# Half of an expert's output product in three rounded products, and bias transfers on another queue

## The reference

```
probs = softmax(x @ gate_w.T);  top2_p, top2_i = top_k(probs, 2)      # 14 experts
w   = top2_p / max(sum(top2_p), 1e-10)
hh  = gelu(x @ w1[e] + b1[e])                                         # w1: 512 x 1024
all_out[e] = hh @ w2[e] + b2[e]                                       # w2: 1024 x 512
result = clip(x + w[:, 0] * all_out[top2_i[:, 0]] + w[:, 1] * all_out[top2_i[:, 1]], -100, 100)
```

## Time and profile before

| what | value |
|---|---|
| runs | 486.13 us median of 3 (485.48 to 486.16) |
| profiled execution | 490.43 us, span from first to last instruction 488.6 us |
| TensorE busy | 452.6 us (93%) |
| VectorE, ScalarE, GpSimd busy | 280.4 us (57%), 162.3 us (33%), 49.8 us (10%) |
| mean granted clock of TensorE | 0.97 of full speed |
| HBM read and written | 93.98 MB and 21.50 MB, 236 GB/s over the span |

### The profile page before, as it was taken

How to read it: one execution, slowest core, us unless ns; L and a number is a source line. 1 busy time by engine, 2 the same in 40 slices (tenths; PEclk the granted TensorE clock), 3 DMA queues, 4 the chain that set the end, 5 groups by cost and what they waited for, 6 DMA issues and landing times.

```text
span 488.6 us, 8054 instructions
## 1 busy us (share of the span) xinstructions
PE 452.6 (93%) x3103; PEld 330.1 (68%) x3112; DVE 280.4 (57%) x555; ACT 162.3 (33%) x314; POOL 49.8 (10%) x58
## 2 busy tenths in 40 slices
PE   2797999999999999997999898999999999999983
PEld 1464665689898999986767766666666666666562
DVE  5639477874363133259565885566665555556637
ACT  4153135133332023043313443423344444333100
POOL 1300000001321111012030420000000000000062
PEclk9989899999999999999998999999999999999987
DMA  8987499004999638000613386899999999984452
GB/s 270 403 322 247 143 395 333 2 1 150 407 406 406 268 132 323 1 3 0 254 52 105 141 260 224 302 331 363 371 345 340 325 349 341 339 323 162 175 160 99
DMA packets 52382, 116.95 MB, mean 239 GB/s; under 512 B 4834, under 2 KB 4850, under 8 KB 52352
## 3 DMA queue, kind: packets, MB, share of 16 engines
q1 hardware_dynamic: 25984, 67.12, 36.8%
q10 hardware_dynamic: 24800, 44.62, 26.2%
q0 software_dynamic: 1568, 4.79, 3.1%
HBM read 93.98 MB, written 21.50 MB: 236 GB/s over the span
## 4 chain that ended last, share of the span: by engine, by line
PE 81%; DVE 12%; issue 2%; DMA 2%; POOL 1%; ACT 1%; DVEq 0%; ACTq 0%; POOLq 0%
PE banks L1780 17%; PE banks L1547 8%; PE banks L1759 5%; PE banks L1761 5%; PE banks L1760 5%; PE banks L1611 4%; PE banks L1413 3%; PE banks L1381 3%; PE banks L1414 3%; PE banks L1415 3%; PE banks L1452 3%; PE banks L1629 2%; PE banks L1400 2%; PE banks L1771 2%; PE banks L1580 2%
## 5 line engine op out<-in xcount | busy, mean ns | idle before, releaser
L1780 PE MATMUL banks<-w,A 128*128 128x512 f32 x208 | 91.4, 592 | 0.0
L670 ACT ACTIVATE A<-banks,b_sb 128x128 f32<-128x128 f32 x112 | 30.5, 383 | 115.5 <-issue 52.8
L1780 PEld LDWEIGHTS banks<-w,A 128*128 128x128 f32 x208 | 38.6, 190 | 43.6 <-issue 43.5
L1285 DVE COPY A<-banks 128x512 f32<-128x512 f32 x28 | 18.0, 686 | 68.0 <-PE banks L1761 67.8
L1213 DVE TENSOR_TENSOR w_lo<-w,w_hi 128x1024 fp32r<-128x1024 f32 x48 | 55.4, 1217 | 0.0
L1547 PE MATMUL banks<-A,w 128*128 128x128 f32 x384 | 48.1, 283 | 0.0
L603 ACT ACTIVATE w_hi<-w 128x1024 fp32r<-128x1024 f32 x48 | 47.3, 1094 | 0.8 <-ACT A L670 0.8
L1547 PEld LDWEIGHTS banks<-A,w 128*128 128x128 f32 x384 | 45.7, 198 | 0.7
L1759 PE MATMUL banks<-w_hi,xr 128*128 128x512 f32 x100 | 40.1, 401 | 1.5 <-DVE xr L1230 1.5
L1760 PE MATMUL banks<-w_lo,xr 128*128 128x512 f32 x104 | 40.5, 389 | 0.0
L1761 PE MATMUL banks<-w_hi,xr 128*128 128x512 f32 x100 | 39.0, 390 | 0.0
(11 more groups left out here) (288 smaller groups left out, 769.4 us busy)
## 6 DMA issues: line engine op xcount, KB each, us to landing
w<-in_w SPq DMA_DIRECT2D x12, 2048.0 KB, 10.1
w<-in_w ACTq DMA_DIRECT2D x12, 2048.0 KB, 10.7
rows_dram<-att ACTq DMA_DIRECT2D x1, 14592.0 KB, 43.1
A<-in_ctxT SPq DMA_DIRECT2D x8, 1024.0 KB, 10.4
A<-in_ctx SPq DMA_DIRECT2D x8, 1024.0 KB, 8.7
w<-in_w SPq DMA_DIRECT2D x6, 1024.0 KB, 6.1
rows_dram<-A ACTq DMA_DIRECT2D x13, 256.0 KB, 3.3
w<-in_wlT SPq DMA_DIRECT2D x3, 1024.0 KB, 15.1
```

Of the source, the lines that this page charges most:

```text
L670: ins = nc.scalar.activation(hT[:, u, f, :], HT[f // 4][:, tile(f % 4)], ACT.Gelu, bias=b1_sb[:, u, f:f + 1])
L1780: ins = mm(YP[:, :], hT[:, u, f, :], w2[:, u, f * D:(f + 1) * D], start=(f == 0), stop=(f == FT - 1))
```

## The change

In `output`, from block 2 on, tiles 4 to 7 of the 8 stay plain fp32 and tiles 0 to 3 (`G = 4`) become three rounded products each, added into the same bank behind the plain ones. For that the first half of `hT` and of `w2` are split: ScalarE rounds them (`high_w2`, and a copy at the end of `gelu`), VectorE subtracts (`low_w2`, `low_h`). In ScalarE's round `high_w2(b-1)` stands between `split_hi(b)` and `store_y(b-2)`; in VectorE's round `low_w2(b-1)` and `low_h(b-1)` stand between `take_y(b-2)` and `take_h(b)`. The issues of `b1` go from SyncE's and ScalarE's programs to GpSimd's, before its gathers.

```diff
+        G = FT // 2
+        w2_hi = [wqkv_lo_flat[:, 0:G * D], c_hi[:, :, :].rearrange("p k n -> p (k n)")[:, 0:G * D]]
+        h_hi = A2r[:, 1024:2048].rearrange("p (u f n) -> p u f n", u=2, f=G)
+        h_lo = A2r[:, 3072:5120].rearrange("p (u f n) -> p u f n", u=2, f=FT)[:, :, 0:G, :]
@@ SyncE @@
-            sp.dma_start(b1_sb[:, 0, :], t["b1T"][0]).then_inc(b1_in[0], 16)
...
-            sp.dma_start(b1_sb[:, 1, :], t["b1T"][1]).then_inc(b1_in[1], 16)
@@ ScalarE @@
+                    if f == G - 1 and not first:
+                        ins.then_inc(gelu_half, 1)
                 ins.then_inc(gelu_done, 1)
+                if not first:
+                    act.wait_ge(gelu_half, b + 1)
+                    nc.scalar.activation(h_hi[:, u], hT[:, u, 0:G, :], ACT.Copy).then_inc(h_high, 1)
+
+            def high_w2(b, u, loaded):
+
+                act.wait_ge(w2_in[u], loaded)
+                for i in range(2):
+                    at = slice(i * G * D // 2, (i + 1) * G * D // 2)
+                    nc.scalar.activation(w2_hi[u][:, at], w2[:, u, at], ACT.Copy).then_inc(w2_high, 1)
...
+            high_w2(2, 0, 32)
             gelu(2, 0, 32)
             pairs = pair_count(act)
             with act.Fori(2, pairs) as i:
                 for u in range(2):
                     split_hi(u, w1_in[u], 16 * i, range(KT))
+                    if u == 0:
+                        high_w2(2 * i - 1, 1, 16 * i)
+                    else:
+                        high_w2(2 * i, 0, 16 * i + 16)
...
-                    act.wait_ge(gelu_done, 2 * i + u - 1)
-                    act.dma_start(b1_sb[:, u, :], t["b1T"][bass.ds(e, 1)].rearrange("o p f -> p (o f)")) \
-                        .then_inc(b1_in[u], 16)
             last = act.value_load(pairs_i[0:1, 1:2], min_val=E // 2 - 1, max_val=MAX_BLOCKS // 2 - 1)
+            high_w2(2 * last + 1, 1, 16 * last + 16)
             store_y(2 * last, 0)
@@ GpSimd @@
+            for u in range(2):
+                pool.dma_start(b1_sb[:, u, :], t["b1T"][u]).then_inc(b1_in[u], 16)
...
+            with pool.Fori(1, pairs) as i:
+                for u in range(2):
+                    e = expert_of(pool, 2 * i + u)
+                    pool.wait_ge(gelu_done, 2 * i + u - 1)
+                    pool.dma_start(b1_sb[:, u, :], t["b1T"][bass.ds(e, 1)].rearrange("o p f -> p (o f)")) \
+                        .then_inc(b1_in[u], 16)
@@ VectorE @@
+            def low_w2(b, u):
+
+                for i in range(2):
+                    dve.wait_ge(w2_high, 2 * b + i + 1)
+                    at = slice(i * G * D // 2, (i + 1) * G * D // 2)
+                    nc.vector.tensor_tensor(w2_lo[:, u, at], w2[:, u, at], w2_hi[u][:, at].bitcast(F32), ALU.subtract) \
+                        .then_inc(w2_low, 1)
+
+            def low_h(b, u):
+                dve.wait_ge(h_high, b + 1)
+                nc.vector.tensor_tensor(h_lo[:, u], hT[:, u, 0:G, :], h_hi[:, u].bitcast(F32), ALU.subtract) \
+                    .then_inc(h_low, 1)
...
+            low_w2(2, 0)
+            low_h(2, 0)
             take_h(3, 1)
...
                     take_y(2 * i + u - 2, u, i)
+                    low_w2(2 * i + u - 1, 1 - u)
+                    low_h(2 * i + u - 1, 1 - u)
                     take_h(2 * i + u, u)
...
+            low_w2(2 * last + 1, 1)
...
             take_y(2 * last, 0, last + 1)
+            low_h(2 * last + 1, 1)
@@ TensorE @@
-                for f in range(FT):
-                    ins = mm(YP[:, :], hT[:, u, f, :], w2[:, u, f * D:(f + 1) * D], start=(f == 0), stop=(f == FT - 1))
+                if isinstance(b, int):
+                    for f in range(FT):
+                        ins = mm(YP[:, :], hT[:, u, f, :], w2[:, u, f * D:(f + 1) * D],
+                                 start=(f == 0), stop=(f == FT - 1))
+                else:
+                    ins = split_output(YP[:, :], b, u, 0, D)
                 ins.then_inc(y_psum, 1)
+
+            def split_output(onto, b, u, at, width):
+                for f in range(G, FT):
+                    mm(onto, hT[:, u, f, :], w2[:, u, f * D + at:f * D + at + width], start=(f == G), stop=False)
+                pe.wait_ge(w2_low, 2 * b + 2)
+                pe.wait_ge(h_low, b + 1)
+                for f in range(G):
+                    cols = slice(f * D + at, f * D + at + width)
+                    mm(onto, h_hi[:, u, f, :], w2_hi[u][:, cols], start=False, stop=False)
+                    mm(onto, h_hi[:, u, f, :], w2_lo[:, u, cols], start=False, stop=False)
+                    ins = mm(onto, h_lo[:, u, f, :], w2_hi[u][:, cols], start=False, stop=(f == G - 1))
+                return ins
...
-                    at = f * D + c * D // 2
-                    ins = mm(HALF[c], hT[:, 1, f, :], w2[:, 1, at:at + D // 2], start=(f == 0), stop=(f == FT - 1))
-                ins.then_inc(half_psum, 1)
+                split_output(HALF[c], 2 * last + 1, 1, c * D // 2, D // 2).then_inc(half_psum, 1)
```

More of the change, by code:

```diff
@@ L269, in perceiver_kernel @@
         y_taken = sem("y_taken")
+        gelu_half, h_high, h_low = sem("gelu_half"), sem("h_high"), sem("h_low")
+        w2_high, w2_low = sem("w2_high"), sem("w2_low")
         y_free = [sem(f"y_free{u}") for u in range(2)]
@@ L662, in _, with gelu @@
                 exp_logits(n)
-            def gelu(b, u, loaded):
+            def gelu(b, u, loaded, first=False):
                 act.wait_ge(hT_psum, b + 1)
@@ L686, in load_w2 @@
                               t["w2"][e].rearrange("(k p) f -> p k f", p=P)).then_inc(w2_in[u], 16)
-            def load_b1(b, e):
-                act.wait_ge(gelu_done, b + 1)
-                act.dma_start(b1_sb[:, b % 2, :], t["b1T"][e]).then_inc(b1_in[b % 2], 16)
             split_hi(0, next_in[0], 16, range(2, KT))
-            gelu(0, 0, 16)
-            load_b1(0, 2)
+            gelu(0, 0, 16, True)
             split_hi(0, w1_in[0], 16, range(2))
@@ L700, in _ @@
             load_w2(0, 2)
-            gelu(1, 1, 16)
-            load_b1(1, 3)
+            gelu(1, 1, 16, True)
+            for count, n in ((gelu_half, 2), (h_high, 2), (w2_high, 4)):
+                act.sem_inc(count, n)
             split_hi(1, w1_in[1], 16, range(2, KT))
@@ L1319, in _ @@
             take_y(1, 1, 1)
+            for count, n in ((h_low, 2), (w2_low, 4)):
+                dve.sem_inc(count, n)
+            low_w2(2, 0)
+            low_h(2, 0)
             take_h(3, 1)
```

## The result

| | before | after |
|---|---|---|
| median of 4 runs each (lowest to highest) | 486.14 us (485.48 to 488.27) | 506.06 us (504.88 to 507.63) |
| ratio, 95% interval | | 1.040 (1.037 to 1.042) |
| profiled execution, its span | 490.43, 488.6 us | 505.67, 504.1 us |
| mean granted clock | 0.97 | 0.96 |

Slower, as forecast, but by 19.9 us instead of 6.8, and outside the range.

What follows compares the result with a forecast made beforehand. TensorE was taken to bound the loop at 13.64 us a block. Loop +0.2 us and tail +6.6 us made +6.8 us; added to the median of 486.13 us, 493.0 us, range 486.5 to 501.5 us.

Steps and rivals of the forecast that it cites:

- the loop's term: Expert loop: w2 waits take back TensorE's saving almost whole, 27.3 us per two blocks against 27.28 before; +0.2 us.
- The circle: ScalarE in the loop: each w2 issue waits for the previous w2 landing, so a step is landing time plus 2.0 us.
- the third rival: Loop transfers crowd: w1 issued 1 to 2 us after w2, w2 lands in about 13.1 us; near 501 us, chance 0.14.
- the loop's upper bound: Loop: at most +3 us if all w2 landings take 12.9 us and TensorE's 1.8 us slack is used up.
- the paragraph on a row and a rule: DMA engines take packets in turn from queues with work; w2, issued 4.4 us ahead, lands later if w1 follows closer.
- TensorE's pace: Loop: three rounded products save 0.18 us a tile, 0.72 us a block; 13.64 to 12.92 us, at best 6.5 us.
- VectorE and ScalarE fit by their sums: Loop: with the added work VectorE has 11.0 us and ScalarE 8.6 us a block, within 12.9 us.
- From landing to the next issue, 2.0 us: ScalarE: row number load 0.75 us, queueing roundings some 0.1 us, store to w2 transfer 1.12 us; together 2.0 us.
- The tail, +6.6 us: After the loop: last block's weights wait for block 13's w2, moving block 12's store from 461.50 to 468.1 us.
- The bias transfers cost nothing: b1 issues on GpSimd have two blocks of time before their gelu; moving them costs nothing and saves nothing.
- The last block's products stay covered: Tail: the work behind block 12's store takes 13 us, still before the gathers' 15.0 us.
- A fall of the clock: Tail only: TensorE's clock at 0.50 early in the halves was included; a longer fall would add up to 1 us.

Runs made afterwards that it cites:

- e3_half_w2: Changed kernel with w2 transfers of 1 MB instead of 2 MB in the loop, all engine instructions kept, output not the layer's: 482.49 us.
- e9_decoupled2: Changed kernel with w2 issued by SyncE behind the next block's w1, gelu before w2's rounding, low_h before low_w2, block 13's low_w2 after block 12's output copy: 479.79 us.
- e4_issue_first: Changed kernel with the rounding of w2 put behind the store and the issue of the next w2 transfer, still ahead of the gelu: 504.05 us.
- e1_tail: Changed kernel with VectorE making the low part of block 13's w2 after the copy of block 12's output, not ahead of the last block's weights: 496.48 us.
- e2_bias_only: Kernel before with only the b1 transfers moved to GpSimd's queue: 486.68 us, ratio 1.000.
- e11_w2_with_w1: Kernel before with b1 transfers on GpSimd's queue and w2 issued together with the next w1 transfer: 490.32 us, ratio 1.005.
- e7_w2_later: Kernel before with w2 issued after the gelu of its round, the bias transfer behind it on the same queue: 500.29 us.
- e12_w2_later: Kernel before with b1 transfers on GpSimd's queue and w2 issued after the gelu of its round: 486.49 us, ratio 0.999.

## Why the prediction was wrong in size

**The step that failed** is the loop's term: "Two blocks then take 10.6 + 2.0 + 12.7 + 2.0 = 27.3 us". The circle and its 2.0 us were right; the landings in it were taken over from the kernel before, as if the new circle left the transfers alone. They measured 13.55 us on average instead of 11.65, and eight of them make 15 us. The forecast of +0.2 us for the loop became +14.3. I had the cause as the third rival, with 0.14, but priced it at 1 us a block, where it took 1.6. Its condition, "w1 is issued only 1 to 2 us after w2", is what the trace shows (1.2 us on average), and the sign named for it, a period over 14.3 us, came.

Two sums were too low by the prediction's own circle. A landing of 13.1 us and 2.0 us make 15.1 us a step, 1.5 us over 13.64 and not 1: nine steps and the tail would have given about 506 us, not 501. And the loop's upper bound of +3 us doesn't follow: landings of 12.9 us throughout make 14.9 us a step, 1.3 us over the old pace, and so 8 us over the loop (eight steps, less the slack of 1.8 us) to 11 us (nine steps). The range ended too low for the cause that it was meant to take in.

What should have told me: the circle changes its own inputs. w2's issue drifts with the landing of the last one while w1's follows TensorE, so the lead of 4.4 us, by which I explained the short landings, was one of the things that the change takes away. My reading of the last three landings in the earlier trace rows was also loose: the first of them (issued at 422.06 us, landed in 9.5 us) does have a w1 transfer behind it, issued 4.5 us later, so single landings scatter even at an equal lead. I had named the mechanism in the paragraph on a row and a rule, and yet kept the old landings for the likeliest case. The Trainium skill (DMA: Bandwidth & Descriptors, section "Queues, rings and completion order") has each DMA engine switch between queues packet by packet; the runs agree in direction (mean landings of 11.5, 13.2, 14.2 us as the lead goes to 0).

The other steps, one by one:

- **TensorE's pace**, 13.64 to 12.92 us: right. e3_half_w2 ran at 12.92 us, e9_decoupled2 at 12.98.
- **VectorE and ScalarE fit by their sums**: true, and too little. e4_issue_first shows a circle through both of 14.77 us, though VectorE's own sum was 11.0 us and ScalarE's 8.6. I never added up a path over two engines. In the change's order it is 12.88 us, level with TensorE's pace: it took nothing here, but only by luck, since I had not looked for it.
- **From landing to the next issue, 2.0 us**: right (335.3 to 337.29 us).
- **The tail, +6.6 us**: +6.4 measured, and 7.3 us back in e1_tail. It has two parts: e3_half_w2's tail step of 16.05 us, with w2 landed in 5.4 us, against e1_tail's 12.34 puts 3.7 us on the order of VectorE's program alone, and the rest on the late transfer.
- **The bias transfers cost nothing**: right (e2_bias_only).
- **The last block's products stay covered**: right, with nothing to spare. They ended later than my 13 us behind the store, at 492.8 us, 15.8 us behind it, and VectorE waited 0.28 us for them, since TensorE had rested 7.64 us for the weights and its granted clock was 0.50 from 477 to 478 us (before, the products with b2 took 3.70 us, now 7.19, and the halves began only behind them, at 484.44 us); but from the store to the end there are still 27.1 us.
- **A fall of the clock**: not in my sum for the loop. After its long rest at 369 to 374 us TensorE resumed at 0.50. It moved that block's output copy (TensorE was 0.75 us behind VectorE), but the copy was over at 383.63 us and w2 landed at 383.7 us, so the circle's step was no longer for it. What it makes of the 14.3 us wasn't measured by itself; the circle of landings accounts for the steps without it.

What stays open: why one landing took 16.4 us with the engines nearly idle for its last two microseconds, and why single landings don't follow the lead. No run here looks inside the DMA engines.

## What to carry to other kernels

Before a wait for a large transfer is put into an engine's program, look at what that engine issues behind it: if it is the next transfer of the same kind, landing time plus a few instructions becomes a lower bound on the pace, and the landings will not stay those of the old profile, since the issue times that made them have moved. Sums of busy time per engine are only a lower bound for a loop's pace; follow one item's path around through every engine until it meets itself, and do so for each order that is considered. A split product that pays 0.7 us a block on TensorE is worth having only with its waits behind the work that others need: the same instructions gave 506 us in one order and 480 us in another.

## What the hardware showed that I had not expected

- Two transfers of 2 MB each on two queues do not suffer alike. Issued together (e11_w2_with_w1), w1, whose rows in HBM are 4 KB, lands in 10.4 to 11.6 us, while w2, with rows of 2 KB, lands in 13.5 to 15.1 us; the last two w2 transfers of the kernel before, with no w1 behind them, took 9.0 and 8.9 us. That the row length makes the difference was not tested. Both on one queue (e9_decoupled2, from 320 us on), w2 lands in 10.3 to 11.3 and w1 in 10.8 to 12.2 us.
- A 4 KB transfer behind a 2 MB one on the same queue lands no sooner than the large one (8.4 to 13.9 us), against 3.5 to 6.5 us on another queue (the changed kernel). In e7_w2_later this cost 13.5 us in all, 500.29 against 486.77; the same issue times without it (e12_w2_later) cost nothing.
- Half of w2's bytes (e3_half_w2), issued 3.5 to 4.1 us ahead of w1, landed in 5.0 us (median), and w1 in 7.6 to 8.3 us. The changed kernel's w2 landed in 13.55 us on average, for twice the bytes.
